# Second layer of a two-layer model on one core: softmax sums beside the maxima on shared wide tiles, and the experts' blocks spread over both

## The reference, cut to what matters

```python
def _L1_attn_ref(x, Wc_down, Wq_up, Wkv_up, Wc_proj):   # 16 heads of 8
    latent = x @ Wc_down
    q = (latent @ Wq_up).reshape(Bsz, Tlen, N_HEAD, HEAD_DIM)
    kv = latent @ Wkv_up
    k, v = (kv[..., :HEAD_DIM], kv[..., HEAD_DIM:])
    att = jnp.einsum('bthd,bsd->bhts', q, k) * scale
    att = jnp.where(causal[None, None], att, -jnp.inf)
    att = jax.nn.softmax(att, axis=-1)
    y = jnp.einsum('bhts,bsd->bthd', att, v).reshape(Bsz, Tlen, C)
    return y @ Wc_proj
...
    for _ in range(LOOPS):                              # 2 loops
        z_norm = _rmsnorm(z, norm_w)
        scores = jax.nn.softmax(z_norm @ router_w, axis=-1)
        topk_vals, topk_idx = jax.lax.top_k(scores, TOP_K)   # 2 of 8
...
        for e in range(E):   # silu(z @ w1) * (z @ w3) @ w2
            mixed = mixed + flat_cw[:, e:e + 1] * _swiglu(flat_z, w1[e], w3[e], w2[e])
        z = z + mixed.reshape(B, S, D)
...
x = x + _L1_attn_ref(xn, ...) + _L1_ffn_ref(xn, ...)
```

## Time and profile before

| | |
|---|---|
| runs | 1918.81, 1920.94 (median), 1928.11 us |
| the profiled execution's own time | 1915.46 us |
| its span | 1914.1 us |
| PE busy | 1588.1 us (83%) |
| DVE, ACT, POOL busy | 1095.6, 938.7, 467.0 us |
| layer 2 | from 829 us to the end |

### The profile page before, as it was taken

How to read it: one execution, slowest core, us unless ns; L and a number is a source line. 1 busy time by engine, 2 the same in 40 slices (tenths; PEclk the granted TensorE clock), 3 DMA queues, 4 the chain that set the end, 5 groups by cost and what they waited for, 6 DMA issues and landing times.

```text
span 1914.1 us, 27776 instructions
## 1 busy us (share of the span) xinstructions
PE 1588.1 (83%) x10720; PEld 725.5 (38%) x10720; DVE 1095.6 (57%) x2036; ACT 938.7 (49%) x1282; POOL 467.0 (24%) x418
## 2 busy tenths in 40 slices
PE   5679888898988997756798978846888999989988
PEld 1233233233323322322355546513554455433323
DVE  4675686679558445869776887766840343231111
ACT  1246565666665674311133324402448655667786
POOL 4002111111112111003381361275154600150000
PEclk8869998998888888755599998857989999999999
DMA  7112221223212221411254453323343533311000
GB/s 224 31 63 71 68 91 64 77 72 96 67 60 81 75 83 54 116 47 43 69 163 113 136 157 105 88 69 114 105 128 97 149 105 103 82 52 40 16 24 12
DMA packets 140788, 163.28 MB, mean 85 GB/s; under 512 B 16336, under 2 KB 99664, under 8 KB 140400
## 3 DMA queue, kind: packets, MB, share of 16 engines
q1 hardware_dynamic: 132320, 144.30, 25.2%
...
## 4 chain that ended last, share of the span: by engine, by line
PE 32%; DVE 14%; ACT 6%; POOL 4%; issue 3%; DMA 1%; SPq 0%; DVEq 0%; ACTq 0%; POOLq 0%
DVE am_top L1598 6%; PE ax_sums L1647 6%; ACT ax_prob L1690 4%; PE sh_bank L2114 4%; PE sh_bank L2150 4%; PE wide L1667 4%; PE sh_bank L2125 3%; PE wide L1566 3%; PE wide L1671 2%; POOL x L2050 2%; DVE am_later L1598 2%; POOL slot_tokens L2036 2%; PE wide L1569 1%; PE sh_bank L1847 1%; PE sh_bank L1725 1%
## 5 line engine op out<-in xcount | busy, mean ns | idle before, releaser
L509 ACT ACTIVATE m_act_h<-m_up,const 128x1024 f32<-128x1024 f32 x256 | 278.3, 1112 | 204.1 <-PE m_up L469 203.5
L1690 ACT ACTIVATE ax_prob<-wide 128x1024 f32<-128x1024 f32 (+3 forms) x384 | 294.8, 811 | 139.6 <-PE wide L1671 111.4
L1598 DVE TENSOR_REDUCE am_top<-wide 128x2 f32<-128x1024 f32 (+3 forms) x256 | 258.2, 1018 | 79.9 <-PE wide L1566 46.4
L1566 PE MATMUL wide<-al_ks,al_qs 48*128 48x512 bf16 (+3 forms) x768 | 150.2, 394 | 127.1 <-DVE am_top L1598 64.9
L555 POOL TENSOR_TENSOR m_prod<-m_prod 128x512 f32<-128x512 f32 x64 | 89.3, 1397 | 516.2 <-DVE m_prod L525 516.2
L2036 POOL DMA_INDIRECT slot_tokens<-mr_zn,mr_slots x128 | 126.2, 986 | 206.7 <-DVE mr_slots L1992 171.0
L469 PE MATMUL m_up<-m_terms,w1s 96*128 96x512 bf16 x512 | 159.5, 409 | 12.9 <-ACT m_act_h L509 12.7
L486 PE MATMUL m_sums<-m_act_h,const 128*32 128x512 f32 x1024 | 147.0, 649 | 27.0 <-DVE m_prod L525 20.5
L2050 POOL DMA_INDIRECT x<-slot_results,mr_slots x128 | 122.5, 957 | 190.1 <-DMA slot_results<-m_y 146.6
L1647 PE MATMUL ax_sums<-ax_prob,al_vs 128*32 128x512 f32 (+3 forms) x1536 | 166.0, 505 | 2.3 <-DVE ax_y L1702 2.3
L1667 PE MATMUL wide<-al_qs,al_ks 51*128 51x512 bf16 (+3 forms) x768 | 126.9, 334 | 28.9 <-ACT ax_prob L1690 27.0
...
## 6 DMA issues: line engine op xcount, KB each, us to landing
...
m_share<-shares SPq DMA_DIRECT2D x128, 256.0 KB
...
```

Source lines behind the costliest of these rows:

```text
L509: A.activation(self.act_h[:, slot, :, :], self.up[u][:, :, :], ACT.Gelu, bias=self.w("b1", 4 * half + ep, 4 * half + ep + 1)).then_inc(sel ...
L1566: p = E.matmul(score[u][:, x, 0:n], *self.keys_queries(i, blk, a, x, seg, n), start=True, stop=True)
L1598: V.tensor_reduce(dst, score[u][:, :, 0:n], AX, ALU.max, negate=True).then_inc(score.read, 1)
L1690: A.activation(self.prob[:, g % 2, 2 * a:2 * a + 2, off:TILE], score[u][:, :, off:TILE], ACT.Exp, scale=SCALE).then_inc(score.read, 1)
```

## The change

Both kinds of use now lie in one plan, `wide_uses`, of 18 places ("slots"). In slot s are the 24 uses of the maxima of task s and, between them one by one, the 24 uses of the sums of task s - 2 (`LEAD = 2`). The wide tiles become a `Shared` set, in which every use has a number and a bank and waits for that bank's own last reader. `SPEED` gives how long a slot is planned: 26 for the first two, 40 until the first block, 53 while there are blocks, 34 after. The blocks of the four phases follow each other without a gap, 8.1 apart instead of 4.2. Every phase is now handled in one way: ACT copies the tokens, takes Tanh and copies the result, and DVE does the two products; POOL has only the indirect transfers. Queries and keys are loaded once for a task, into 4 slots, and the maxima's rows are loaded by a generator of their own. `ax_prob` has 3 buffers in place of 2.

```diff
-MAX_TASK, SUM_TASK, SUM_START = 24.0, 22.0, 392.0
-ROUTE = [0.0, 45.0, 236.0, 336.0]
-SCATTER = [r + 38.0 for r in ROUTE]
-BLOCKS = [84.0, 186.0, 320.0, 424.0]
-STEP = 4.2
-EARLY = 3
+STEP = 8.1
+MOVED = GATHER * 2 * GT
+BLOCKS = [84.0 + (STEP * NBLK + 3.0) * ph for ph in range(len(PHASES))]
+COMBINE = [start + STEP * NBLK + 4.5 for start in BLOCKS]
+ROUTE = [0.0, 45.0] + [COMBINE[ph] + MOVED + 4.0 for ph in range(len(PHASES) - GROUPS)]
+SCATTER = [start + 38.0 for start in ROUTE]
...
+SPEED = [(0.0, 26.0), (52.0, 40.0), (BLOCKS[0], 53.0), (BLOCKS[-1] + STEP * NBLK, 34.0)]
+LEAD = 2
...
 def max_at(i, x):
-    return MAX_TASK * (i + x)
+    return slot_at(i + x)
 def sum_at(i, x):
-    return SUM_START + SUM_TASK * (i + 0.95 * x)
+    return slot_at(i + LEAD + x)
...
+def wide_uses():
+    uses, n, m = {}, len(MAX_USES), 2 * len(SUM_STEPS)
+    for i in range(TASKS):
+        uses |= {("max", i, u): max_at(i, u / n) for u in range(n)}
+        uses["turn", i] = max_at(i + 1, (AHEAD - 0.25) / n)
+        uses |= {("sum", i, u): sum_at(i, (u + 0.5) / m) for u in range(m)}
+    return uses
...
-            uses["t", ph, b], uses["a", ph, b], uses["b", ph, b], uses["y", ph, b] = at - 1.6, at, at + 0.9, at + STEP + 0.45
+            uses["t", ph, b], uses["a", ph, b], uses["b", ph, b], uses["y", ph, b] = at - 1.6, at, at + 1.5, at + STEP + 0.75
...
+    Q_SLOTS = 4
...
-        for t in range(2 * TASKS):
+        for i in range(TASKS):
...
+    def sync_maxima(self, amax):
+        S, s = self.k.nc.sync, self.k.sp
+        for i in range(TASKS):
+            yield amax.turn_place(i) + 9.0
+            s.wait_ge(amax.sent[i % 2], 48 * (i // 2 + 1))
...
-        self.prob, self.y = sb("prob", 2, HG, TILE), sb("y", 2, NG, T)
+        self.prob, self.y = sb("prob", 3, HG, TILE), sb("y", 2, NG, T)
...
-                    e.wait_ge(*self.amax.score.done(len(self.amax.number) - 1))
-                    e.wait_ge(*score.free(u))
+                    e.wait_ge(*wide.free("sum", i, u))
...
-            V.tensor_scalar(self.sum[:, :], self.sum[:, :], 1.0, 1.0 if ph < EARLY else 2.0, ALU.add, ALU.mult).then_inc(step, 1)
+            V.tensor_scalar(self.sum[:, :], self.sum[:, :], 1.0, 2.0, ALU.add, ALU.mult).then_inc(step, 1)
...
-                if ph < EARLY:
-                    A.activation(self.act_h[n % 2][:, :], shared.bank("a", ph, b)[:, :], ACT.Silu).then_inc(*shared.empties("a", ph, b))
...
-                    A.activation(self.hid[n % 2][:, :], shared.bank("b", ph, b)[:, :], ACT.Copy).then_inc(*shared.empties("b", ph, b))
-                else:
-                    A.activation(self.act_h[n % 2][:, :], shared.bank("a", ph, b)[:, :], ACT.Tanh, scale=0.5).then_inc(self.tanh_made, 1)
+                A.activation(self.act_h[n % 2][:, :], shared.bank("a", ph, b)[:, :], ACT.Tanh, scale=0.5).then_inc(self.tanh_made, 1)
...
-                G.tensor_tensor(self.hid[n % 2][:, :], self.act_h[n % 2][:, :], self.hid[n % 2][:, :], ALU.mult).then_inc(self.hid_made, 1)
```

251 lines of the change are left out of this document (103 added, 148 removed).

## The result

The changed kernel takes **1901.16 us** (median of 4 runs, 1898.52 to 1902.66) beside 1920.81 us of the kernel before (4 runs, 1918.81 to 1928.11): a ratio of 0.9889, 95% interval 0.9861 to 0.9917. That is faster by 1.1%, where 4.0% was forecast, and 1.2 us above the upper end of the range.

What follows compares the result with a forecast made beforehand. DVE was taken to bound up to the first block, PE between blocks, the open gather after: 829 + 108 + 844 + 57 = 1838 us of span, forecast 1845 us as median, range 1800 to 1900 us.

Steps and rivals of the forecast that it cites:

- The end: After the last block: the last gather lies open, then closing work; 57 us, with PE idle for half of it.
- The stalls of the earlier trace: Two single PE waits, 20.4 us, while DVE stood in combinations whose gather was not there yet; claimed to go.
- Part 2, the waits of TensorE: Between first and last block: PE loses 63 us to waits, beside 781 us of work, 844 us in all.
- the two terms: Between first and last block: 35 us from 50 gaps with little filling, 28 us from DVE products ahead of reductions.
- Part 2, TensorE's work: Between first and last block: 781 us of PE work at full clock, 8.5 us for each of 92 blocks.
- the rival that I had put beside it: Fills of maxima on wide tiles: short waits return, clock falls as in the 0.86 row; 2023 us in total, chance 0.08.
- Part 1: From 829 us to the first block: DVE bounds, 16 fewer reductions save 15 us, 108 in place of 123.
- dearer coupling: Mixed stretch: late Tanh holds DVE's product and the reduction behind it, PE at 87%; total 1899 us, chance 0.17.
- the Tanh as the releaser in most blocks: Mixed stretch: ACT's Tanh releasing DVE's products in most blocks would show the forecast wrong.

Runs made afterwards that it cites:

- tanh_free: Changed kernel with ScalarE's Tanh run on constants into a tile aside, so VectorE's first product waits for TensorE alone: 1898.2 us, 0.9868 of the kernel before.
- snapped53: Changed kernel with the experts' four pieces placed on the grid of the fills, same work and average pace: 1848.55 us, 0.9637 of the kernel before.

## Why the prediction was off

**The end (57 us).** Right: 54.9. The gather lies open, 3.2 us behind the border of the window, and the divisions and additions follow as listed.

**The stalls of the earlier trace rows.** Right: 2.74 us is the longest wait that is left.

**Part 2, the waits of TensorE (63 us).** This is the step that failed, though not in the two terms that it held: it left out waits of 42.6 us. I counted 50 gaps with only a sum's fill between, at 0.7 us each, 35 us, and 28 us for DVE's products ahead of reductions. The trace has 45 such gaps with 28.8 us, and all waits for reductions come to 53.6 us. That the second term came out near its size (24.8 us in all other gaps) does not show its cause: no run moved DVE's products alone, and tanh_free, in which they no longer wait for ScalarE, left these waits as they were. Missing are the waits that I gave no term: for exponentials 17.8 us (the earlier trace rows had 27.0 of them), for "issue" (nothing that the profile shows) 7.1, for a block's rows 7.1, for its first product's bank 5.4, for the turning of the maxima 3.2 and 2.0, together 42.6. TensorE's idle time is 99.6 us, not 63.

**Part 2, TensorE's work (781 us).** 14 us too low, 795.1: I took it at full clock, and the clock was 0.95. From 1447 to 1527 us it was 0.81. I also took it for fixed, and it depends on the order: in snapped53 the same instructions take 762.0 us. The Trainium skill ("TensorE: Matmul & The Clock Gate", "A second HAM failure mode: psum-queue depth-cycling") has TensorE's short pauses between groups push the clock up and down. By that rule, the trace agrees in small: 0.95 with 99.6 us of pauses and 0.99 with 73.0, but nothing like the 0.86 of the rival that I had put beside it.

**Part 1 (108 us).** "DVE bounds there, and one reduction costs 0.945 us: 16 fewer save 15 us." They left (DVE 104.4 to 90.9 us busy), and the time stayed. Windows up to the first scatter and from it to the first block, of before and then of the change:

```profile
829.00:884.80 55.80, 38.12 (x183) 18.32 (x183) 46.20 (x102) 7.08 (x13) 0.00 (x0) 0.50 0.07 17
884.80:952.00 67.20, 45.20 (x210) 19.99 (x208) 58.18 (x118) 7.32 (x12) 34.68 (x34) 0.50 0.24 71
```

```profile
829.00:885.10 56.10, 36.26 (x171) 17.68 (x171) 44.10 (x98) 7.08 (x13) 0.03 (x1) 0.50 0.10 23
885.10:951.70 66.60, 52.42 (x280) 18.64 (x280) 46.82 (x100) 22.75 (x30) 34.98 (x35) 0.55 0.20 63
```

Up to the scatter little changed. Behind it DVE fell from 87% to 70% busy and TensorE rose from 67% to 79%, at a clock of 0.55, near the lower level of 1.2 GHz. So what failed here is "DVE bounds" as the reason for a price of 0.945 us for each reduction less. My reading, which is argued and not shown, is that the chain of a fill at the low clock and its reduction bounds now. Shorter reductions (-20 us) and fewer uses ahead of the block (-9 to -12) shorten it; more of TensorE's work lengthens it by no more than two traces of one kernel differ. How it divides between the two engines stays open.

**The rival.** What came is the "dearer coupling" (1899 us, PE at 87%) by its number, with PE at 89%. That is luck: its mechanism, the late Tanh that holds DVE's product and the reduction behind it, is refuted by tanh_free. I had named the Tanh as the releaser in most blocks as a sign; it was the releaser in 46 of 92, and removing that wait moved nothing.

**The largest miss** is none of the numbers: I took the 63 us of waits for a property of two tiles in turn. They depend on the places given to the work. With the same instructions at other places the kernel is at 1848.6 us, with TensorE 91% busy, near the forecast of 1845. 26.6 us of that gain are idle time of TensorE, and 33.1 us are the same work in less time, a term that I had not thought of at all.
